# A graph layer's last stages on one core: finish and routing of the last layer as one stage over seven groups of blocks

## The reference

```
def gcn_conv(x, W, b, src, dst, n):          # called twice; below, the second
    h = x @ W
    dinv = rsqrt(in-degree + 1)
    agg = segment_sum(h[src] * dinv[src] * dinv[dst], dst) + h * dinv**2
    return agg + b
h2 = relu(gcn_conv(h1, W2, b2, src, dst, n))  # W2: 64 x 256
x = x + h2 + mix(xn)
...
def ffn(h):                                   # h = layernorm(x)
    logits = h @ gate_w + gate_b              # 8 experts
    probs = softmax(logits); idx = argmax(probs); prb = probs[idx]
    one_hot = one_hot(idx)
    pos = (cumsum(one_hot, axis=0) * one_hot).sum(-1) - 1
    kept = pos < C                            # C = 977
    buf[idx, pos] = h (if kept)
    y = relu(buf @ w1 + b1) @ w2 + b2
    return y[idx, min(pos, C - 1)] * prb * kept
x = x + ffn(layernorm(x))
```

## Time and profile before

| | us |
|---|---|
| median of 3 runs | 5758.02 |
| their lowest and highest | 5753.02, 5766.75 |
| the profiled execution | 5764.05 |
| its span in the profile | 5762.3 |

### The profile page before, as it was taken

The page is one execution under the profiler, slowest core; times in us unless marked ns, Lnnn a source line. Parts: engine busy times, 40 slices in busy tenths (PEclk is TensorE's granted clock), DMA queues, the critical chain, the costliest instruction groups (busy, mean ns, idle before and its releaser), DMA issues. The chain is left out here.

```text
span 5762.3 us, 68520 instructions
## 1 busy us (share of the span) xinstructions
PE 3544.4 (62%) x13636; PEld 2691.9 (47%) x13637; DVE 2995.2 (52%) x6650; ACT 1002.2 (17%) x2108; POOL 3048.8 (53%) x2954
## 2 busy tenths in 40 slices
PE   3755556554399760599635555554555555583998
PEld 3633334333277550377534444443544545461665
DVE  5367777777899762144453444444333333442443
ACT  0022222221399510122110000000000000021111
POOL 1167777774288525100367777776777777503111
PEclk9867777776699875799755666665555555556999
DMA  5477777774288542521241111112111111122220
GB/s 199 96 208 231 234 231 229 236 230 148 88 272 271 171 158 72 166 64 64 79 114 32 32 33 32 33 33 42 32 33 32 32 33 33 24 74 83 95 74 31
DMA packets 430920, 630.36 MB, mean 109 GB/s; under 512 B 100204, under 2 KB 307838, under 8 KB 429383
## 3 DMA queue, kind: packets, MB, share of 16 engines
q1 hardware_dynamic: 298907, 375.58, 20.5%
q0 software_dynamic: 107056, 200.91, 14.7%
q10 hardware_dynamic: 24876, 53.00, 2.6%
HBM read 419.56 MB, written 222.20 MB: 111 GB/s over the span
## 5 line engine op out<-in xcount | busy, mean ns | idle before, releaser
L1846 POOL DMA_INDIRECT big<-t_d,src_tiles x1564 | 1493.0, 955 | 551.0 <-issue 463.0
L2069 PE MATMUL v_bank<-big,v_oh 128*128 x3328 | 682.9, 391 | 928.1 <-POOLq L1842 857.3
L2069 PEld LDWEIGHTS v_bank<-big,v_oh 128*128 128x128 f32 x3328 | 650.3, 299 | 1004.0 <-issue 1004.0
L642 POOL DMA_INDIRECT big<-xl_d,src_steps x832 | 833.2, 1001 | 302.6 <-issue 244.7
L1924 DVE TENSOR_TENSOR big<-big,v_bank 128x64 f32 x1664 | 367.7, 221 | 1148.4 <-PE v_bank L2069 914.3
L738 PE MATMUL se_z_ps<-big,se_oht 128*128 x1664 | 654.1, 553 | 482.0 <-DVE se_z L685 174.1
L738 PEld LDWEIGHTS se_z_ps<-big,se_oht 128*128 128x128 f32 x1664 | 424.6, 272 | 711.1 <-issue 623.8
L685 DVE TENSOR_TENSOR se_z<-se_z_ps,big 128x528 f32<-128x528 f32 x416 | 291.7, 701 | 353.9 <-DMA big<-xl_d,src_steps 284.2
L955 POOL TENSOR_TENSOR ae_v<-ae_v,ex 128x1792 f32<-128x1792 f32 x104 | 334.5, 3219 | 236.6 <-DMA ae_v<-xj_d 236.3
L996 PE MATMUL ae_bank<-ae_v,ae_oh 128*128 128x266 f32 x1664 | 402.9, 397 | 49.7 <-DVE big L980 37.1
L996 PEld LDWEIGHTS ae_bank<-ae_v,ae_oh 128*128 128x128 f32 x1664 | 310.1, 191 | 142.3 <-DVE big L980 53.3
(11 more groups left out here) (401 smaller groups left out, 5174.4 us busy)
## 6 DMA issues: line engine op xcount, KB each, us to landing
xj_d<-big SPq DMA_DIRECT2D x208, 528.0 KB, 3.2
ae_v<-xj_d SPq DMA_DIRECT2D x208, 528.0 KB
se_dlb<-dlr_d SPq DMA_DIRECT2D x104, 256.0 KB, 5.0
big<-t_d,src_tiles POOLq DMA_INDIRECT x1564
buf_d<-e_blank ACTq DMA_DIRECT2D x4, 4112.0 KB, 36.2
e_xs<-buf_d SPq DMA_DIRECT2D x106, 128.0 KB
y_d<-e_y SPq DMA_DIRECT2D x106, 128.0 KB
big<-xl_d,src_steps POOLq DMA_INDIRECT x832
```

The costliest lines, as they stand in the source:

```text
L642: nc.gpsimd.indirect_dma_start(half_of(u)[:, k, :], None, table, bass.IndirectOffsetOnAxis(ap=m.src[:, t:t + 1], axis=0)).then_inc(landed[ ...
L1846: nc.gpsimd.indirect_dma_start(rows[:, t % RING, :], None, table, bass.IndirectOffsetOnAxis(ap=m.srct[:, t:t + 1], axis=0)).then_inc(lande ...
L2069: last = nc.tensor.matmul(bank[u][:, k * MH:(k + 1) * MH], oh[:, u, k, :], of_block(rows, at[k]), start=True, stop=True)
```

## The change

One stage, `finish_and_route1`, takes the place of `finish_convolution`, the barrier, and `route` for layer 1. The 49 blocks are seven groups of seven. In step g of eight, the finish of group g stands beside the gate and routing of group g-1. `us` and `ut` are 128 columns and rows wide, the rest zeros (the ones for the bias are column 64 of `us` and come through the turn); `w2` has 128 rows. The normalised rows are made once, in `disp`, and used for the gate and for the send. Choosing and counting go by group, on arrays of 128x56; the counts are carried from group to group. All loops are written out. `big0` is laid out anew so that the expert weights can be loaded while `m.agg` is still read.

```diff
@@ finish_convolution and route(layer 1) -> finish_and_route1 @@
+        G = 7
+        NGR = NB // G
+        w2, ut, us = sb("w2", [P, D]), sb("ut", [P, 4, P]), sb("us", [P, 4, P])
...
             def _(sp):
+                sp.wait_ge(s["ones"], 2)
                 sp.dma_start(w2[0:MH, :], a["L1_gnn_W2"]).then_inc(s["weights"], 16)
                 sp.dma_start(w2[MH:MH + 1, :], a["L1_gnn_b2"].rearrange("(a n) -> a n", a=1)).then_inc(s["weights"], 16)
+                sp.dma_start(wg[:, :, :], a["L1_ffn_gate_w"].rearrange("(c p) n -> p c n", p=P)).then_inc(s["weights"], 16)
+                sp.dma_start(bg[:, :], a["L1_ffn_gate_b"].partition_broadcast(P)).then_inc(s["weights"], 16)
+                for g in range(NGR):
+                    b0, b1 = G * g, min(G * g + G, NB - 1)
+                    sp.wait_ge(s["res_ready"], G * (g + 1))
+                    sp.dma_start(m.out[b0 * P:b1 * P, :].rearrange("(b p) d -> p b d", p=P), m.acc[:, b0:b1, 0:D]).then_inc(s["res_out"], 16)
...
             def _(pool):
...
+                for g in range(NGR):
+                    pool.wait_ge(s["r_ready"], G * (g + 1))
+                    pool.wait_ge(s["t_ready"], g + 1)
+                    pool.wait_ge(s["p_ready"], g + 1)
+                    pool.wait_ge(s["slots"], g + 1)
+                    for i in range(G):
+                        k = G * g + i
+                        nc.gpsimd.indirect_dma_start(m.buf1_d, bass.IndirectOffsetOnAxis(ap=m.slots[:, 0, k:k + 1], axis=0),
+                                                     disp[:, g % 2, i, :], None, bounds_check=m.buf1_d.shape[0] - 1,
+                                                     oob_is_err=False).then_inc(sent[g % 2], 16)
...
             def _(dve):
-                V.memset(ut[MH:MH + 1, :, :], 1.0).then_inc(s["ones"], 1)
+                V.memset(us[:, :, MH:P], 0.0).then_inc(s["ones"], 1)
+                V.memset(w2[:, :], 0.0).then_inc(s["ones"], 1)
+                dve.wait_ge(s["ones"], 2)
+                V.memset(us[:, :, MH], 1.0).then_inc(s["ones"], 1)
...
+                def normalise(g):
+                    part = slice(G * g, G * g + G)
+                    dve.wait_ge(s["std"], g + 1)
+                    c.did(V.reciprocal(m.rstd[:, part], m.tmp1[:, part]))
+                    if g >= 2:
+                        dve.wait_ge(sent[g % 2], 16 * G * (g // 2))
+                    V.tensor_copy(disp[:, g % 2, :, RW - 1], token[:, part]).then_inc(s["t_ready"], 1)
+                    c.sync()
+                    for i in range(G):
+                        k = G * g + i
+                        V.tensor_scalar(disp[:, g % 2, i, 0:D], rows_of(k), m.mean[:, k:k + 1], m.rstd[:, k:k + 1],
+                                        ALU.subtract, ALU.mult).then_inc(s["xn_ready"], 1)
...
+                for g in range(NGR + 1):
+                    if g < NGR:
+                        for k in range(G * g, G * g + G):
+                            if k + 5 < NB:
+                                scale(k + 5)
+                            finish(k)
+                            if k > G * g:
+                                stats(k - 1)
+                        stats(G * g + G - 1)
+                        variance(g)
+                    if g >= 1:
+                        choose(g - 1)
+                    if g < NGR:
+                        normalise(g)
+                    if g >= 1:
+                        place(g - 1)
...
             def _(act):
+                for e in range(2):
+                    load_expert_weights1(act, m, a, e, e, s["experts"])
...
+                for g in range(NGR + 1):
+                    for k in range(G * g, G * g + G):
+                        if k + 4 < NB:
+                            turned(k + 4)
+                        if g >= 1:
+                            normal_turned(k - G)
+                            residual(k - G)
+                    if g < NGR:
+                        act.wait_ge(s["var"], g + 1)
+                        nc.scalar.activation(m.tmp1[:, G * g:G * g + G], m.tmp0[:, G * g:G * g + G], ACT.Sqrt).then_inc(s["std"], 1)
+                    if g >= 1:
+                        act.wait_ge(s["l_in"], g)
+                        nc.scalar.activation(gap[:, :, :], gap[:, :, :], ACT.Exp).then_inc(s["exped"], 1)
...
             def _(pe):
...
+                pe.wait_ge(s["weights"], 64)
+                pe.wait_ge(s["ones"], 3)
+                for k in range(4):
+                    turn(k)
+                project(0)
+                for g in range(NGR + 1):
+                    for k in range(G * g, G * g + G):
+                        if k + 4 < NB:
+                            turn(k + 4)
+                        if k + 1 < NB:
+                            project(k + 1)
+                        if g >= 1:
+                            turn_normal(k - G)
+                            if k > G * g:
+                                gate(k - G - 1)
+                    if g >= 1:
+                        gate(G * g - 1)
+                        pe.wait_ge(s["counted"], g)
...
+                        nc.tensor.matmul(ranks(g - 1), tri[:, :], flat, start=True, stop=True)
+                        nc.tensor.matmul(totals(g - 1), m.ones[:, :], flat, start=True, stop=True).then_inc(s["totals"], 1)
@@ weights1, experts1, memory: big0 @@
-    m.table = m.big0[:, 0:NB * MH].rearrange("p (b n) -> p b n", n=MH)
-    m.agg = m.big0[:, NB * MH:2 * NB * MH].rearrange("p (b n) -> p b n", n=MH)
+    m.agg = m.big0[:, 0:NB * MH].rearrange("p (b n) -> p b n", n=MH)
+    m.table = m.big0[:, NB * MH:2 * NB * MH].rearrange("p (b n) -> p b n", n=MH)
```

More of the change, by code:

```diff
@@ L2133, in _, with finish_and_route1, rows_of, gates @@
                     pipeline(pe, NR, 1, even, (1, down, NB), (0, up, NB), odd)
-def finish_convolution(nc, m, a):
+def finish_and_route1(nc, m, a):
     with ExitStack() as ctx:
         def sb(name, shape, dt=F32):
[L2141 to L2146, removed]
+            return ctx.enter_context(nc.sbuf_tensor("fr_" + name, shape, dt))
+        G = 7
+        NGR = NB // G
+        w2, ut, us = sb("w2", [P, D]), sb("ut", [P, 4, P]), sb("us", [P, 4, P])
+        wg, bg = sb("wg", [P, KC, NE]), sb("bg", [P, NE])
+        xt, disp = sb("xt", [P, 4, D]), sb("disp", [P, 2, G, RW])
+        score, mask, cand, gap = (sb(n, [P, G, NE]) for n in ("score", "mask", "cand", "gap"))
+        best, least, sf = sb("best", [P, G]), sb("least", [P, G]), sb("sf", [P, G])
+        tot, incl = sb("tot", [P, NE, G]), sb("incl", [P, 2, NE, G])
+        notfirst, start, limit = sb("notfirst", [P, NE, G]), sb("start", [P, NE]), sb("limit", [P, NE])
+        valid, absent = sb("valid", [P, NB]), sb("absent", [P, NB])
+        token, tri = sb("token", [P, NB]), sb("tri", [P, P])
+        bank = [ctx.enter_context(nc.psum_tensor(f"fr_bank{i}", [P, 512], F32)) for i in range(8)]
+        s = {n: m.sem("fr_" + n) for n in ("weights masks ones u_ready ut_made ut_ready made res_ready stat chain var std xn_ready "
+                                           "xt_made xt_ready g_made g_back l_in exped counted totals t_ready p_ready r_ready slots "
+                                           "sent0 sent1 experts res_out").split()}
+        sent = [s["sent0"], s["sent1"]]
+        def rows_of(k):
+            return m.acc[:, k, 0:D]
+        def gates(g):
+            return bank[6][:, 64 * (g % 2):64 * (g % 2) + G * NE].rearrange("p (b e) -> p b e", e=NE)
+        def ranks(g):
+            return bank[7][:, 128 * (g % 2):128 * (g % 2) + G * NE]
+        def totals(g):
+            return bank[7][:, 128 * (g % 2) + 64:128 * (g % 2) + 64 + G * NE]
         with nc.Block() as block:
@@ new lines, in _ @@
+                for k in range(5):
+                    scale(k)
+                dve.wait_ge(s["masks"], 10)
+                c.did(V.tensor_scalar(absent[:, :], valid[:, :], -1.0, -1.0e6, ALU.add, ALU.mult))
+                for g in range(NGR + 1):
[14 more added lines that the diff above has]
+                        place(g - 1)
@@ L2192, in project @@
+                def project(k):
                     pe.wait_ge(s["ut_ready"], k + 1)
-                    if at_least(k, 2):
+                    if k >= 2:
                         pe.wait_ge(s["res_ready"], k - 1)
[L2195 to L2198, removed]
+                    nc.tensor.matmul(bank[2 + k % 2][:, 0:D], ut[:, k % 4, :], w2[:, :], start=True, stop=True).then_inc(s["made"], 1)
@@ new lines, in turn_normal, with gate @@
+                def turn_normal(k):
+                    pe.wait_ge(s["xn_ready"], k + 1)
+                    if k >= 2:
+                        pe.wait_ge(s["xt_ready"], k - 1)
+                    for q in range(KC):
+                        last = nc.tensor.transpose(bank[4 + k % 2][:, q * P:(q + 1) * P],
+                                                   disp[:, k // G % 2, k % G, q * P:(q + 1) * P], m.ident[:, :])
```

(11 more changed lines are left out.)

148 lines of the change are left out of this document (124 added, 24 removed).

## The result

| | before | after |
|---|---|---|
| median of 4 runs of each, us | 5755.52 | 5676.00 |
| lowest and highest | 5748.75, 5766.75 | 5666.89, 5680.61 |
| the profiled execution, its span | 5764.05, 5762.3 | 5677.77, 5676.1 |
| the two stages, or the one: DVE's first memset to the experts' first DMA | 249.5 | 173.95 |
| experts' first DMA to the span's end | 490.6 | 490.7 |

The ratio is 0.9858, 95% interval 0.9837 to 0.9879: faster by 79.5 us, where 5680 was forecast. The stage is 75.5 us shorter and the experts as long as before. The other 10.7 us between the two profiled executions lie ahead of the stage, in code that differs only in two addresses of `big0`.

What follows compares the result with a forecast made beforehand. Work of PE, DVE and POOL lying end to end was taken as the bound; start, first piece, six cycles of 20 and a 26.7 tail save 78.0 us, giving 5686, or 5680 as median; range 5660 to 5718.

Steps and rivals of the forecast that it cites:

- three pieces side by side: Finish, gate work and POOL's sends, 89, 67 and 72 us end to end, would overlap; experts begin 78.0 us earlier.
- cycle: Finish of one group beside the gate of the previous one, six times: put at 20 us each.
- first piece: Finish of group 0 alone at the new stage's start, forecast to end at 5047.
- merged block: PE's turn, product, transposes and gate records for 128 nodes: 2.46 us at the low clock, 1.35 at the high.
- tail: After the six cycles: last gates, choose, counting, place, sends, until the experts' first DMA: 26.7 us.
- Padding at the low clock: Full tiles in the finish would cut a turn and product from 1.75 to 1.29 us a block.
- Rival 3: Padding gives nothing in mixed work: block 3.13 us, cycle 28.3, kernel 5730; chance 0.08.
- The clock: PE's granted clock within each cycle: two blocks low and four high, since PE's idle makes each cycle begin low.
- rival 1: The clock never rises in the merged stage: cycle 24.3 us, 25.8 more, kernel 5706; chance 0.25.
- Rival 2: Clock stays high or rises at once, small loads land early: cycle 18.7, start 4.5 sooner, kernel 5668; chance 0.15.
- DVE's tail: DVE's choose, normalise and place behind a group's last gate: 1.95, 2.75 and 3.4 us.
- The second chain: DVE's wait for POOL's sends from the reused buffer, then normalise and place: an 18.7 us floor under the cycle.

Runs made afterwards that it cites:

- merge_only: The changed kernel with the partial tiles of before (64-column turns, 65-row products): 5704.74 us, ratio 0.9929 to the kernel before.
- pad_only: The kernel before with only the finish's turns and products padded to 128, stages still apart: 5708.51 us, ratio 0.9932 to the kernel before.
- kept_busy: The changed kernel plus unread products (four and eight of 256 columns) where PE waits for DVE in each cycle: 5659.65 us, stage 160.3.
- small_first: The changed kernel with the expert weights' loads held back until the four small loads have landed: 5669.99 us, stage 171.3.
- three: The changed kernel with three send buffers instead of two: 5672.57 us, stage 174.4.
- pool_delayed: The changed kernel with two POOL memsets on an unused buffer ahead of each group's sends: 5709.72 us, stage 199.8.

## Why the prediction was right

The forecast case came, by the mechanism that was forecast: three pieces side by side, a cycle of two chains of like length, a clock that moves within it. That the total came so near is in part luck, since errors in its terms cancel. Against its terms (profiled execution):

| step | forecast | measured |
|---|---|---|
| stage shorter by | 78.0 | 75.5 |
| PE's first turn after the stage's start | 9.3 | 9.7 |
| end of the first piece after the stage's start | 25 | 23.3 |
| merged block, low and high clock | 2.46, 1.35 | 2.56, 1.32 |
| choose, normalise and place | 8.1 | 6.9 |
| from the first send to its group's landing seen | 11.4 | 13.1 |
| cycle | 20 | 20.7 (19.4 to 21.6) |
| tail | 26.7 | 26.5 |

- **Three pieces side by side**: right. The tail, which nothing covers, was right to 0.2 us, and the experts did not change. The first piece was 1.7 shorter, since the clock rose in its third block already (0.91 from 5025 to 5030) and DVE then paced it, and the six cycles were 4.1 longer: 124.1 instead of 120.
- **Padding at the low clock**: 1.28 against 1.29 forecast in the finish. Rival 3 fell: the padded block is 2.56, not 3.13. The Trainium skill's sentence that a matmul on 32 rows takes the time of one on 128 (TensorE: Matmul & The Clock Gate, Why this matters for your kernels) leads to no gain; for turns of 64 columns and products of 65 rows, one behind the other, the trace shows the partial pair slower, 1.75 against 1.28, at one clock, with a share at each of the two shapes (0.16 and 0.13 of 0.29 in the merged block).
- **The clock**: right in kind, too hopeful in size. "Two blocks low and four high" came in one cycle (first turn at 5056.3; the sends then held it). The others had three and three, about four and two, nearly five and one (twice), and all low in the last. So rival 1 came true in that last cycle and fell for the others; merge_only has its 0.50 throughout, but with partial tiles. The Trainium skill's rule that transposes do not count as a busy PE (same page, Part 4: PE-mode transpose) agrees with the route's 0.50 in pad_only, 57.98 of 60 us busy. Beside padded turns and products the same transposes did not keep the clock down; in the last cycle, with padded products but hardly a turn, it stayed down. Which of these the clock follows is open.
- **Rival 2** (clock high, small loads early) had the cycle at 18.7 and the stage 12.3 shorter than forecast; kept_busy and small_first show what its two halves would have been worth, 13.6 and 2.7.
- **DVE's tail** was overpriced by 1.2: the operations of 56 elements take 0.21 and follow at 0.25. This and the longer time at the low clock partly cancel: with three blocks low a cycle is 0.3 + 11.6 + 0.8 + 6.9 = 19.6, where the forecast had 19.5 with two low and the dearer tail. That is luck, and the right total does not show it.
- **The second chain** was underpriced by 2.0 (landing 4.3 and the start 1.5, for 2.55 and 1.25). What DVE does behind the wait was overpriced by 1.0, so the chain came to 19.6 and not 18.7. It stayed just below the first, as forecast, and passed it in one cycle (1.76 of waiting).
- The stage gave 2.5 us less than forecast and the median came 4 lower than forecast; the difference is in what lies ahead of the stage, and says nothing on it.
- **Small slips in its arithmetic**: seven sends are 8.83 and not 8.85, and the last gates end 3.7 into the tail and not 3.8. The 0.11 a record behind part of the 1.35 is not what the earlier trace rows divide to (0.13 and 0.125, which would make about 1.45); the measured 1.32 is nearer to the forecast than to its source.

What the prediction missed is the size of what was left: each of the clock's fall and the sends hides part of what the other costs, and 28 us more lay behind the two together.

## What to carry to other kernels

When stages bound by different engines lie end to end, merge them group by group, and price the cycle by its chains: the busy sums (16 us of PE at these clocks, 13 of DVE) say less than the one engine that idles behind another's serial tail. Look at what a tile's shape does to the clock as well as to its own time: here zeros in half a tile were worth 0.3 to 0.47 us a block by themselves and more through the clock. And when two chains of like length bound a cycle, an experiment that shortens one alone can show nothing (three: 0, where the same buffer gave 15 more beside kept_busy's products); shorten both before calling either harmless. Check a right total by its parts, too: here, and in pool_delayed, it came out of terms that were off by several us each.

## What the runs showed of the hardware that I had not expected

- A stream of partial tiles (64 columns of weights, then 65 rows) left the granted clock at 0.50 for 89 us with PE busy 96% of them, and for the whole merged stage of merge_only. The padded stream in its place had 0.90 from 2 to 7 us after its first turn (pad_only, second window).
- Full tiles are not enough for the clock to rise: in the last cycle of the changed kernel PE was full for 13 us, with padded products among transposes and gate products, at 0.50.
- More work on PE shortened the stage: 144 more matmul records, 13.6 us less (kept_busy, one run).
- POOL's memset slows DVE beside it. Timeline of DVE in pool_delayed while the memset (5062.31 to 5067.65) runs:

```profile
5062.49 2.52 DVE L2236 TENSOR_SCALAR fr_us<-big,dinv 128x64 f32<-128x64 f32 x1
5062.65 2.37 DVE L2240 SCALAR_TENSOR_TENSOR big<-fr_bank,big 128x256 f32<-128x256 f32 x1
5062.99 2.03 DVE L2244 BATCH_NORM_STATS2 st<-big 128x6 f32<-128x256 f32 x1
```

These take 0.25, 0.42 and 0.42 elsewhere in the same run. It does not enter the chain read off above, which is POOL's and the DMAs' until 5081.02, but DVE's busy time in that cycle is 16.1 us instead of 13.4.
